# RWKV layer: x added inside TensorE's accumulator, dummy matmuls ahead of some stages, new orders

## The reference

```
xn = LN(x); sx = shift(xn) - xn
xxx = tanh((xn + sx * maa_x) @ maa_w1)                # 5 groups of 32
x5[n] = xn + sx * (maa_stack[n] + xxx[n] @ maa_w2[n]) # n = w, k, v, r, g
w = exp(-exp(time_decay + tanh(x5[w] @ dw1) @ dw2))
r, k, v = x5[r] @ Wr.T, x5[k] @ Wk.T, x5[v] @ Wv.T;  g = silu(x5[g] @ Wg.T)
per token: out = r * (u * k v + s);  s = k v + w * s  # per head, 8 x 8 state
att = groupnorm(out) * gn_w + gn_b
x2  = x + (att * g) @ Wo.T
xn2 = LN(x2); xk, xr = mixes of xn2 and its shift
out = x2 + sigmoid(xr @ Fr.T) * (square(relu(xk @ Fk.T)) @ Fv.T)
```

## Time and profile before

| | |
|---|---|
| median of 3 runs | 539.96 us (539.35 to 544.64) |
| the profiled execution | 541.4 us, its span 539.6 us |
| busy: VectorE, TensorE, ScalarE, POOL | 482.4, 460.1, 284.3, 91.2 us |
| granted TensorE clock, mean | 0.918 of full speed |
| DMA | 69.34 MB, mean 129 GB/s |

### The profile page before, as it was taken

The page is one execution under the profiler, slowest core; times in us unless marked ns, Lnnn a source line. Parts: engine busy times, 40 slices in busy tenths (PEclk is TensorE's granted clock), DMA queues, the critical chain, the costliest instruction groups (busy, mean ns, idle before and its releaser), DMA issues.

```text
span 539.6 us, 5791 instructions
## 1 busy us (share of the span) xinstructions
PE 460.1 (85%) x1968; PEld 257.4 (48%) x1968; DVE 482.4 (89%) x530; ACT 284.3 (53%) x614; POOL 91.2 (17%) x93
## 2 busy tenths in 40 slices
PE   0786889899799988999799979999899969954857
PEld 0463554464356344654365436544465536532435
DVE  0457999999999999989999999999999999999474
ACT  5353177378526844665636852765456263633533
POOL 0001011211420041010332042113202121101020
PEclk9996989899989996998899988999799979985888
DMA  8271291688377827980798357772796069711020
GB/s 267 95 193 21 84 223 30 155 200 187 61 183 162 188 40 171 205 199 2 139 211 207 67 79 182 171 183 54 159 223 151 2 126 226 153 40 30 0 39 30
DMA packets 26726, 69.34 MB, mean 129 GB/s; under 512 B 1608, under 2 KB 19656, under 8 KB 24264
## 3 DMA queue, kind: packets, MB, share of 16 engines
q1 hardware_dynamic: 19448, 54.55, 40.6%
q0 software_dynamic: 7248, 14.42, 15.8%
HBM read 46.15 MB, written 12.19 MB: 108 GB/s over the span
## 4 chain that ended last, share of the span: by engine, by line
PE 51%; issue 22%; DVE 11%; ACT 9%; POOL 5%; DMA 1%; SPq 0%; DVEq 0%; ACTq 0%; POOLq 0%
PE pa L843 13%; PE pc L850 10%; PE pc L843 4%; PE patt L984 4%; PE pb L910 3%; POOL out L403 2%; PE pc L835 2%; PE pb L953 2%; DVE kv L534 2%; DVE x L459 2%; PE pa L881 2%; PE pa L938 2%; POOL rs L384 1%; ACT ob L673 1%; PE pb L869 1%
## 5 line engine op out<-in xcount | busy, mean ns | idle before, releaser
L534 DVE TENSOR_TENSOR_SCAN kv<-w_sb,kv 128x512 f32<-128x512 f32 (+2 forms) x144 | 147.1, 1083 | 0.1
L843 PE MATMUL pa<-x,large_sb 128*128 128x512 f32 (+2 forms) x288 | 129.2, 596 | 2.2 <-DVE x L468 1.7
L843 PEld LDWEIGHTS pa<-x,large_sb 128*128 128x128 f32 x288 | 59.0, 212 | 62.4 <-issue 49.4
L542 DVE TENSOR_TENSOR kv<-kv,r_sb 128x2048 f32<-128x2048 f32 (+2 forms) x36 | 73.7, 2048 | 0.4
L524 DVE TENSOR_TENSOR kv<-vrep,k_sb 128x2016 f32<-128x2016 f32 (+2 forms) x36 | 71.8, 2012 | 0.2 <-PE patt L984 0.2
L394 POOL COPY kv<-s_sb 128x32 f32<-128x32 f32 (+2 forms) x36 | 34.6, 963 | 189.8 <-PE patt L984 171.5
L881 PE MATMUL pb<-th,w_sb 32*128 32x512 f32 (+2 forms) x108 | 40.8, 681 | 18.7 <-DVE x L459 18.7
L459 DVE SCALAR_TENSOR_TENSOR x<-pb,vec_sb,sx 128x512 f32<-128x512 f32 (+2 forms) x72 | 46.1, 681 | 7.0 <-PE pb L881 4.8
L363 POOL DMA_DIRECT2D x<-xn x21 | 19.7, 936 | 177.9 <-DVE x L459 177.9
L639 ACT ACTIVATE ob<-xres 128x256 f32<-128x256 f32 x29 | 11.7, 405 | 52.1 <-DVE xres L567 52.1
L984 PE MATMUL patt<-kv,const_sb 128*32 128x512 f32 (+2 forms) x288 | 36.4, 578 | 0.1
(11 more groups left out here) (128 smaller groups left out, 779.3 us busy)
## 6 DMA issues: line engine op xcount, KB each, us to landing
vrep<-v_scratch SPq DMA_DIRECT2D x12, 2048.0 KB, 13.7
x<-xn POOLq DMA_DIRECT2D x18, 512.0 KB, 7.4
vrep<-v_scratch SPq DMA_DIRECT2D x4, 1536.0 KB, 10.7
x_tok<-in_x SPq DMA_DIRECT2D x6, 512.0 KB, 9.6
v_scratch<-v_sb SPq DMA_DIRECT2D x12, 256.0 KB
xres<-in_x SPq DMA_DIRECT2D x6, 512.0 KB, 4.2
out<-xres SPq DMA_DIRECT2D x6, 512.0 KB, 13.9
out<-trr POOLq DMA_DIRECT2D x6, 512.0 KB, 7.0
```

The costliest lines, as they stand in the source:

```text
L534: ins = dve.tensor_tensor_scan(flat, w_sb[:, p, q % HF, 0:nb].rearrange("p b t -> p (b t)"), flat, 0.0, ALU.mult, ALU.add)
L542: dve.tensor_tensor(flat, flat, r_sb[:, p, q % HF:q % HF + 1, 0:n].broadcast_to([P, G4, n]), ALU.mult).then_inc(rs_ready, 1)
L843: ins = pe.matmul(dst[:, m, 0:n], w(a)[:, m * P:(m + 1) * P], src[:, a, :], start=(a == 0), stop=(a == HF - 1))
```

## The change

- `res` leaves VectorE. WO first multiplies each tile of `xres` (x) by the identity into the accumulator, then adds the two products with Wo. WO waits for the load of x (`res_in`) as well.
- ScalarE's first pass of `st2` reads the accumulator, writes x2 to `xres` and sums it in the same operation; a further tiny operation scales the sums to the mean. For the three last parts ScalarE copies only, and VectorE's `bn_stats` follows.
- `warm` puts dummy matmuls (identity times 256 columns of constants, into an accumulator that is free at that point) ahead of some stages, by the table `WARM`; in all but the first of them behind a wait that says that the accumulator is free.
- All orders are new, and each engine has a list for the start (`..._HEAD`) too. The tails (not shown) move single stages: in VectorE's, `gate 7` goes ahead of `sc0 8` and the `res` go; in TensorE's, KK 9 and RR 10 are exchanged, and KK 10 goes ahead of Y2 8.

```diff
-DVE_ORDER = [("rs1", 3), ("shift2", 4), ("mix4", 2), ("sc2", 3), ("a3", 3), ("rs2", 3), ("sc3", 3), ("rs3", 3),
-             ("rk", 2), ("out", 4), ("a0", 2), ("shift", 1), ("bonus", 2), ("sc0", 2), ("gate", 3), ("rs0", 2),
-             ("mix0", 1), ("mix1", 1), ("res", 3), ("a1", 2), ("a2", 2), ("mix2", 1), ("sc1", 2), ("mix3", 1)]
-PE_ORDER = [("X01", 1), ("BO", 2), ("WO", 3), ("S0", 2), ("P0", 1), ("X2", 1), ("X3", 1), ("T2", 3), ("P1", 1),
-            ("X4", 1), ("S1", 2), ("RR", 3), ("D1", 1), ("KK", 3), ("D2", 1), ("P3", 1), ("S2", 2), ("Y2", 3),
-            ("T1", 0), ("S3", 2), ("CB", 1), ("VR", 2), ("P4", 1), ("W1", 0)]
-ACT_ORDER = [("w", 2), ("r", 2), ("xn", 1), ("sq", 3), ("rstd", 3), ("tg", 2), ("th", 1), ("st", 0),
-             ("st2", 3), ("v", 1), ("nrm2", 3), ("xn2", 3), ("k", 1), ("rr", 3), ("thd", 1), ("nrm", 0),
-             ("kk", 3)]
-POOL_ORDER = [("s02", 3), ("s03", 3), ("ad4", 2), ("s00", 2), ("ad0", 1), ("s01", 2), ("ad1", 1), ("rd1", 0),
-              ("ay", 4), ("rd2", 3), ("ad3", 1)]
-SP_ORDER = [("vl1", 4), ("vst", 3), ("lx", 1), ("vl0", 3), ("sx2", 5), ("lr", 4)]
+DVE_ORDER = [("a3", 3), ("sc2", 3), ("sc3", 3), ("rs2", 3), ("rs3", 3), ("rk", 2), ("out", 4), ("a0", 2),
+             ("shift", 1), ("bonus", 2), ("sc0", 2), ("gate", 3), ("rs0", 2), ("mix0", 1), ("mix1", 1),
+             ("a1", 2), ("mix2", 1), ("sc1", 2), ("mix3", 1), ("rs1", 2), ("a2", 2), ("shift2", 3), ("mix4", 1)]
+PE_ORDER = [("BO", 2), ("X2", 1), ("P0", 1), ("X3", 1), ("S0", 2), ("T2", 3), ("X4", 1), ("P1", 1), ("S1", 2),
+            ("RR", 3), ("D1", 1), ("KK", 3), ("D2", 1), ("P3", 1), ("Y2", 3), ("S2", 2), ("T1", 0), ("S3", 2),
+            ("CB", 1), ("VR", 2), ("P4", 1), ("W1", 0), ("X01", 0), ("WO", 2)]
+ACT_ORDER = [("tg", 2), ("th", 1), ("st", 0), ("st2", 3), ("v", 1), ("nrm2", 3), ("xn2", 3), ("k", 1),
+             ("rr", 3), ("nrm", 0), ("thd", 1), ("kk", 3), ("w", 1), ("r", 1), ("xn", 0), ("sq", 2),
+             ("rstd", 2)]
+POOL_ORDER = [("s02", 3), ("ad4", 2), ("s03", 3), ("ad0", 1), ("s00", 2), ("ay", 4), ("rd1", 0), ("ad1", 1),
+              ("s01", 2), ("rd2", 3), ("ad3", 1)]
+SP_ORDER = [("lx", 3), ("vl0", 5), ("vl1", 5), ("sx2", 6), ("vst", 4), ("lr", 5)]
 SUBS = 3
...
+DVE_HEAD = [("shift", 0), ("mix0", 0), ("mix1", 0), ("mix2", 0), ("mix3", 0)]
+PE_HEAD = [("T1", 0), ("W1", 0), ("X01", 0), ("P0", 0), ("X2", 0), ("X3", 0), ("P1", 0), ("X4", 0), ("D1", 0),
+           ("D2", 0), ("P3", 0), ("CB", 0), ("T1", 1), ("P4", 0), ("W1", 1)]
+ACT_HEAD = [("st", 0), ("nrm", 0), ("xn", 0), ("th", 0), ("st", 1), ("v", 0), ("k", 0), ("thd", 0), ("nrm", 1)]
+POOL_HEAD = [("rd1", 0), ("ad0", 0), ("rd1", 1), ("ad1", 0), ("ad3", 0)]
+SP_HEAD = [("lx", 0)]
+WARM = {("KK", 1): 6, ("RR", 7): 5, ("RR", 9): 1, ("T1", 0): 16, ("T2", 2): 6, ("T2", 3): 6, ("T2", 4): 6,
+        ("T2", 5): 6, ("T2", 6): 6, ("T2", 7): 14, ("T2", 9): 3, ("W1", 0): 6, ("WO", 0): 6, ("WO", 8): 6,
+        ("X01", 0): 2}
+LAGS = 6
...
-def schedule(table, tail):
-
-    return [(name, i - lag) for i in range(NCH + LAGS) for name, lag in table
-            if 0 <= i - lag < NCH and (name, i - lag) not in tail] + tail
+def schedule(head, table, tail):
+
+    return head + [(name, i - lag) for i in range(NCH + LAGS) for name, lag in table
+                   if 0 <= i - lag < NCH and (name, i - lag) not in head + tail] + tail
...
-            def c_res(k, _):
-                c, at, n = part(k)
-                dve.wait_ge(wo_done, k + 1)
-                dve.wait_ge(res_in, 16 * (c + 1))
-                res = xres[:, tile_span(k), :]
-                dve.tensor_tensor(res, res, product_tok(k)[:, 0:n // P], ALU.add).then_inc(x2_ready, 1)
 
...
+                variance(count, over, src, mean, var, scratch, mean_ready, squared, var_ready)
+
+            def variance(count, over, src, mean, var, scratch, mean_ready, squared, var_ready):
+
                 act.wait_ge(mean_ready, count)
...
             def c_moments(k, _):
+                act.wait_ge(wo_done, k + 1)
                 if k >= LAST:
+                    act.activation(xres[:, tile_span(k), :], product_tok(k)[:, 0:1], ACT.Copy).then_inc(x2_ready, 1)
                     return
+                if k >= 1:
+
+                    act.wait_ge(t2_done, k)
+                    act.wait_ge(xhat2_ready, k)
+                for t in tiles(k):
+                    ins = act.activation(xres[:, t, :], product_tok(k)[:, t], ACT.Copy, accum_out=sh2[:, t:t + 1])
+                ins.then_inc(x2_ready, 1)
                 act.wait_ge(x2_ready, k + 1)
-                if k >= 1:
-
-                    act.wait_ge(t2_done, k)
-                moments(k + 1, k, tiles(k), xres, mean2, var2, xhat2, mean2_ready, squared2, var2_ready, xhat2_ready)
+                n = tile_span(k)
+                act.activation(mean2[:, n], sh2[:, n], ACT.Copy, scale=-1.0 / E).then_inc(mean2_ready, 1)
+                variance(k + 1, tiles(k), xres, mean2, var2, xhat2, mean2_ready, squared2, var2_ready)
 
             def normalize(count, over, src, mean, rs, sh, dst, scale_ready, shift_ready, done):
...
+            def warm(name, k, dst, free, count):
+
+                if WARM.get((name, k)):
+                    if count:
+                        pe.wait_ge(free, count)
+                    for _ in range(WARM[name, k]):
+                        pe.matmul(dst[:, 0, 0:2 * P], ident, const_sb[:, 0:2 * P], start=True, stop=True)
+
...
             def wo(k, _):
+                warm("WO", k, product(k), ln_ready, part(k)[0] + 1)
                 if k == 0:
                     pe.wait_ge(in_late, 16)
                 pe.wait_ge(y_ready, k + 1)
+                pe.wait_ge(res_in, 16 * (part(k)[0] + 1))
                 if k == PARTS - 1:
                     pe.wait_ge(gated, LAST)
-                project_tok(k, lambda a: weight("Wo", a), att, wo_done)
+                for i, t in enumerate(tiles(k)):
+                    pe.matmul(product_tok(k)[:, i], ident, xres[:, t, :], start=True, stop=False)
+                    for a in range(HF):
+                        ins = pe.matmul(product_tok(k)[:, i], att[:, a, t * P:(t + 1) * P], weight("Wo", a), start=False, stop=(a == HF - 1))
+                ins.then_inc(wo_done, 1)
 
...
             def t2(k, _):
+                warm("T2", k, product(k), x2_ready, k + 1)
                 pe.wait_ge(xhat2_ready, k + 1)
                 transposes(tiles(k), product(k), xhat2, t2_done)
 
```

More of the change, by code:

```diff
@@ new lines @@
+POOL_ORDER = [("s02", 3), ("ad4", 2), ("s03", 3), ("ad0", 1), ("s00", 2), ("ay", 4), ("rd1", 0), ("ad1", 1),
+              ("s01", 2), ("rd2", 3), ("ad3", 1)]
+SP_ORDER = [("lx", 3), ("vl0", 5), ("vl1", 5), ("sx2", 6), ("vst", 4), ("lr", 5)]
+SUBS = 3
+DVE_TAIL = [("rs1", 7), ("shift2", 6), ("sc2", 7), ("a3", 7), ("mix4", 8), ("sc3", 7), ("rs2", 7), ("rs3", 7),
+            ("rk", 8), ("out", 6), ("a0", 8), ("a1", 8), ("bonus", 8), ("gate", 7), ("sc0", 8), ("rs0", 8),
+            ("sc1", 8), ("a2", 8), ("sc2", 8), ("rs1", 8), ("rs2", 8), ("shift2", 7), ("a3", 8), ("sc3", 8),
+            ("rs3", 8), ("gate", 8), ("out", 7), ("gate", 9), ("gate", 10), ("st2", 8), ("st2", 9),
+            ("nrm2", 8), ("st2", 10), ("nrm2", 9), ("shift2", 8), ("nrm2", 10), ("shift2", 9), ("shift2", 10),
+            ("out", 8), ("out", 9), ("out", 10)]
@@ L60 @@
-POOL_TAIL = [("s02", 7), ("s03", 7), ("ad4", 8), ("s00", 8), ("s01", 8), ("ay", 6), ("s02", 8), ("rd2", 7),
-             ("s03", 8), ("ay", 7), ("rd2", 8), ("rd2", 9), ("ay", 8), ("rd2", 10)]
-SP_TAIL = [("vl1", 6), ("sx2", 5), ("vst", 7), ("vl0", 7), ("vl1", 7), ("lr", 6), ("vst", 8), ("vl0", 8),
-           ("vl1", 8), ("sx2", 6), ("lr", 7), ("sx2", 7), ("lr", 8), ("sx2", 8)]
-LAGS = 5
+           ("RR", 9), ("KK", 8), ("RR", 10), ("KK", 9), ("KK", 10), ("Y2", 8), ("Y2", 9), ("Y2", 10)]
+ACT_TAIL = [("r", 8), ("w", 8), ("sq", 7), ("rstd", 7), ("st2", 7), ("nrm2", 7), ("xn2", 7), ("tg", 8),
+            ("rr", 7), ("sq", 8), ("kk", 7), ("rstd", 8), ("st2", 8), ("st2", 9), ("st2", 10), ("xn2", 8),
+            ("xn2", 9), ("xn2", 10), ("rr", 8), ("rr", 9), ("rr", 10), ("kk", 8), ("kk", 9), ("kk", 10)]
@@ new lines @@
+POOL_TAIL = [("s02", 7), ("s03", 7), ("s00", 8), ("ad4", 8), ("ay", 6), ("s01", 8), ("s02", 8), ("rd2", 7),
+             ("s03", 8), ("ay", 7), ("rd2", 8), ("rd2", 9), ("ay", 8), ("rd2", 10)]
+SP_TAIL = [("vl1", 6), ("sx2", 5), ("lr", 6), ("vst", 7), ("vl0", 7), ("vl1", 7), ("vst", 8), ("sx2", 6),
+           ("vl0", 8), ("lr", 7), ("vl1", 8), ("sx2", 7), ("lr", 8), ("sx2", 8)]
+DVE_HEAD = [("shift", 0), ("mix0", 0), ("mix1", 0), ("mix2", 0), ("mix3", 0)]
+PE_HEAD = [("T1", 0), ("W1", 0), ("X01", 0), ("P0", 0), ("X2", 0), ("X3", 0), ("P1", 0), ("X4", 0), ("D1", 0),
+           ("D2", 0), ("P3", 0), ("CB", 0), ("T1", 1), ("P4", 0), ("W1", 1)]
@@ L626, in _ @@
                 **{f"rs{q}": (lambda c, p, q=q: b_read(c, p, q)) for q in range(NQ)},
```

(7 more changed lines are left out.)

22 lines of the change are left out of this document (7 added, 15 removed).

## The result

The median of 4 runs is 536.13 us (531.33 to 537.41) against 540.77 of the kernel before beside it: ratio 0.9885 [0.9838, 0.9932], in brackets the 95% interval. In a second measurement it took 534.4 (528.01 to 535.49), ratio 0.9856 [0.9800, 0.9912]. A few executions of some kernels lie over 1.5% above the fastest of the same kernel, and the medians and ratios leave them out. The forecast was 528.4 with a spread of its own from 521 to 533, and the whole range went to 539: the time lies in the range, on its slow side, and outside the forecast's own spread. The profiled execution took 531.33 us, the shortest of its four (forecast 529.8), so its trace shows the change at its best.

The account below looks back on a forecast made before the run. VectorE was taken to set the pass, with TensorE close behind. Gains of 7.0 + 1.2 + 0.5 + 2.9 = 11.6 us off the 540.0 median gave 528.4 us, own spread 521 to 533, whole range to 539.

Parts of the forecast that it names:

- (c): Start: the 16 dummies run at half speed to the end, T1 8.1 us late with nothing won; 536.5 us, chance 0.07.
- (b): Middle passes: the clock falls around T2's transposes only, whatever stands before them; T2 and P1 stay slow; 538.1 us, chance 0.13.
- the first 132 us: Up to the middle passes: start net nothing, X2 before P0 shortens waits, no wait for v; 0.5 us gained together.
- five passes: Loop from 132.09 to 421.46 us: each pass of 57.87 us gets 1.4 us shorter, 7.0 us in all.
- the sixth stretch: Up to 474.84 us, VectorE's alone, ending in TensorE's wait for the gate: one add less, 1.2 us.
- the end: Chunk 7 and last parts: WO stays cold, 1.8 us longer; dummies speed T2 and RR; 2.9 us gained, ends -1 and 5.
- The add and the identity matmul: Each full chunk: VectorE gets back 1.21 us, floor 55.6 us a pass; WO takes 1.81 us more on TensorE.
- TensorE becomes the bound at 56.5 us: Middle passes: waits before X3 and T2 go, TensorE's loop is 56.5 us against VectorE's 55.9, a narrow bound.
- I expect the full clock to hold: Middle passes: only tanh's idle stretch is left, so X3, T2 and P1 run at full rate; 2.9 us of TensorE back.
- The start: Chunk 0: 16 dummies make T1 3.6 to 4.9 us late, full speed wins some 4.5 us; net nothing, ends -4 and +3.
- (a): Middle passes: the clock still falls, now before the dummies, which run at half speed; loop 62.1 us, total 556 us, chance 0.08.
- (d): Middle passes: a new wait of about 1 us each, at nrm2, a2 or W1; 533.4 us, chance 0.12.

## Why the prediction was right, and where it was off

The range and the sign held, and the mechanism did in the middle of the kernel. The median forecast was 7.7 us too low, 6.0 by the second measurement, and 536.13 is as near to rivals (c), 536.5, and (b), 538.1, as to anything: only the trace tells them apart. The profiled execution came within 1.5, with luck: it had the best clock of its four. By the forecast's own terms, in the profiled execution: the first 132 us -2.7 (+0.5 forecast), five passes 3.55 (7.0), the sixth stretch 2.1 (1.2), the end 7.2 (2.9): 10.1 against 11.6, with errors that cancel. (Two inner cuts of the earlier trace rows, 190.00 and 248.19, are not starts of X01, which stand at 186.92 and 247.22; the sum and the mean of 57.87 don't depend on them.) Step by step:

- **The add and the identity matmul: right.** One operation of 1.21 us less per chunk on VectorE, 1.7 us (four times 0.43) more on TensorE (1.81 forecast). VectorE's busy time in a full pass is 56.07 us, 0.5 over the 55.6 forecast. No wait of WO for the load of x shows, and ScalarE's passes out of PSUM take 0.383 us each, as taken.
- **TensorE becomes the bound at 56.5 us: right** (56.73). X3, T2, P1, the missing waits before X3 and before `out`: all as forecast. From X01(4) to X01(8) the gain is 6.8 and 8.4 us in the two profiles of the changed kernel, where four times 1.4 was forecast.
- **"I expect the full clock to hold": too strong.** It holds in many passes and not in all; it fell behind the wait of 1.21 us before WO at 137.97, and at 194.80 behind no more than tanh's. A kernel whose TensorE has no slack hands each fall on, 1.6 to 1.9 us a pass (58.41 us against 56.77 in the second run, 58.11 against 56.20 with SP's old orders, the shorter ones at a clock of 1.00), and the spread from 528 to 537 us goes with the clock. The run that took 528.01 had a clock of 0.997; the medians of the two measurements are 0.974 and 0.984, 4 to 7 us by 3.1 us per 0.01. That is the size of the whole miss, though the terms below were off too and cancel in part.
- **The first 132 us and what follows: the step that failed.** "Both halves of v are then issued no later than now, and no wait for them shows in VectorE's list: nothing." I had moved P0 behind X2 a few sentences earlier, and given WO, ahead of both, more work and dummies, and noted that ScalarE's `v` comes later, but followed that delay only to nrm2, not to the store, the load and a0. The first half was issued 26.5 us after X01 instead of 20.1; only the second was earlier. It cost 6.3 us of waiting. The text had named the fault as a condition ("only if the store ahead of it held v back"), but with the wrong cause: the store of x2 at 92.41 was gone long before. The late P0 and a store that landed 2.6 us later made 3.6 to 3.9 us of the wait (what is left with SP's old orders), and the joint issue of the halves most of the rest. 0.5 us of gain for the first 132 us turned into 2.7 of loss. The first of the five passes, where 1.4 us were to be won, lost 3.3 more (54.8 to 58.1). With SP's old orders it takes 56.2 at a clock of 1.00, with VectorE busy for 56.06 instead of 54.66: so some 1.4 us is work that moved into it, and the other 1.9, at a clock of 0.94, is the step on the clock above. In the second run of the changed kernel the first 142 us lost 10.0 us and this pass nothing (54.8).
- **The start: right in its net.** The 16 dummies took 8.68 us for 32 records, mostly full speed, not half; T1 came at 12.89 (13.6 to 14.9 forecast), P0 in 1.99 us. X01(1) is 1.9 us earlier in the two profiles with the best clock and 0.3 to 1.0 us later in the other seven of the new orders with start dummies: nothing, within the ends given.
- **The end: under-sized**, 7.2 us after WO 7 instead of 2.9. The term "stays cold, and becomes 1.8 us longer" was wrong: the wait ahead was 1.69 us instead of 3.03, and WO did not start cold. After the gate of part 8 another 2.6 us came instead of 0.5. From X01(8) on, the orders alone take 118.6 us, the identity alone 117.1, both without dummies 112.2, all 108.9 (118.1 before): in these profiles, one of each kernel, orders and identity need each other.
- **Rival (b): fell.** T2's eight transposes take 1.04 us amid full-speed work and P1 behind them 3.60, in each of the full passes at clock 1. (The rule weighed there, the Trainium skill, "TensorE: Matmul & The Clock Gate", section "Part 4: PE-mode transpose", is not borne out for the rate of these f32 transposes in the full passes at clock 1; whether they count as activity no run here tests.) **Rival (a)** is real, but only with the old orders (1.013). **Rival (c)** fell. **Rival (d)**, a new wait: TensorE waits 6.1 us for `bonus` (W1) in the whole span, none of it in the full passes at clock 1, and VectorE 12.3 us for X2 and X3, 0.5 in each of those passes; the new wait that counted was the one for v, not in the list.

What stays open: why the load of v follows its store by 12 us in the third pass instead of 9.4, under either of SP's orders; what P0's place alone costs; and why the clock falls in one pass and not in another behind the same wait of 1.90 us. A version with P0 ahead of X2 again was not run. The best measured is the changed kernel with SP's old orders, 0.9753 and 0.9820, below both kernels in both measurements.
